# A four-stage transformer kernel: second attention in one product per head, additions moved between engines, a different preparation and heavier fillers

## The reference, cut to what matters

```python
x = x + tanh(g_xattn[0]) * attention_0(ctx, ctx, layernorm(x))   # 16 heads, softmax over the HEADS
x = x + tanh(g_ffn[0])   * ffn_0(layernorm(x))                   # silu(x Wg) * (x Wu), then Wd; hidden 768
x = x + tanh(g_xattn[1]) * attention_1(layernorm(x), ctx)        # 16 query heads, one k and v of width 16
x = x + tanh(g_ffn[1])   * ffn_1(layernorm(x))                   # x (W + low rank).T + b
# attention_1:
q = (x @ Wq) split into 16 heads of 16;  k, v = split(ctx @ Wkv, 2)
att = softmax(q k.T / 4, over the 120 context rows);  y = (att @ v) joined;  return y @ Wo
```

## Time and profile before

| | |
|---|---|
| median of three runs | 2813.01 us (2812.63 to 2813.55) |
| the profiled execution | 2812.17 us, of which its span is 2810.4 us |
| TensorE busy | 95% of the span |
| VectorE busy | 88% |
| ScalarE busy | 56% |
| GpSimd busy | 51% |
| granted TensorE clock over the span | 0.987 |

### The profile page before, as it was taken

How to read it: one execution, slowest core, us unless ns; L and a number is a source line. 1 busy time by engine, 2 the same in 40 slices (tenths; PEclk the granted TensorE clock), 3 DMA queues, 4 the chain that set the end, 5 groups by cost and what they waited for, 6 DMA issues and landing times.

```text
span 2810.4 us, 75822 instructions
## 1 busy us (share of the span) xinstructions
PE 2656.1 (95%) x30576; PEld 2278.9 (81%) x30576; DVE 2469.6 (88%) x4425; ACT 1563.9 (56%) x3125; POOL 1427.9 (51%) x1591
## 2 busy tenths in 40 slices
PE   3799999999999999999999999999999999999996
PEld 2688888888888888888888888888888888888884
DVE  4589999999999999999999999999999999999973
ACT  3355555555555555555555555555555555555553
POOL 1454465465455455456456446546545545545630
PEclk9799999999999999999999999999999999999997
DMA  2000000000000000000000000000000000000000
GB/s 76 24 22 25 26 25 29 23 27 28 21 28 27 21 30 25 21 30 25 25 27 25 25 26 27 28 21 27 28 21 30 25 21 30 25 21 30 25 16 9
DMA packets 74668, 73.15 MB, mean 26 GB/s; under 512 B 6907, under 2 KB 73745, under 8 KB 74642
## 3 DMA queue, kind: packets, MB, share of 16 engines
q1 hardware_dynamic: 74642, 72.80, 8.5%
HBM read 54.94 MB, written 16.78 MB: 26 GB/s over the span
## 4 chain that ended last, share of the span: by engine, by line
PE 36%; DVE 25%; POOL 24%; issue 6%; ACT 3%; DMA 2%; SPq 2%; POOLq 1%; DVEq 0%
POOL zt L345 8%; PE work L1081 8%; POOL h_lo L342 8%; PE work L1203 7%; PE work L1083 6%; PE work L1082 6%; DVE m L821 5%; POOL zt L349 4%; PE scores L1173 3%; DVE x L836 3%; POOL zt L352 2%; DVE y1f L833 2%; DVE e L830 2%; ACT e L509 2%; DMA x_ln<-xp 2%
## 5 line engine op out<-in xcount | busy, mean ns | idle before, releaser
L509 ACT ACTIVATE e<-scores 120x1024 f32<-120x1024 f32 x512 | 504.6, 1024 | 178.7 <-PE scores L1183 163.8
L342 POOL TENSOR_TENSOR h_lo<-h_f,h_hi 128x256 fp32r<-128x256 f32 x384 | 401.9, 1061 | 192.4 <-ACT h_hi L468 192.4
L1081 PE MATMUL work<-xt_hi_B,w_hi 128*128 128x256 f32 x1536 | 442.4, 288 | 0.9 <-DVE h_f L811 0.5
L1082 PE MATMUL work<-xt_lo_B,w_hi 128*128 128x256 f32 x1536 | 429.4, 280 | 0.0
L1083 PE MATMUL work<-xt_hi_B,w_lo 128*128 128x256 f32 x1536 | 428.5, 279 | 0.0
L830 DVE TENSOR_TENSOR e<-e,rz 120x2048 f32<-120x2048 f32 x128 | 383.8, 2998 | 2.2
L345 POOL TENSOR_TENSOR zt<-e 120x512 f32<-120x512 f32 x256 | 332.0, 1307 | 57.4 <-ACT e L509 57.4
L817 DVE TENSOR_REDUCE m<-scores 120x128 fp32r<-120x2048 f32 x128 | 293.3, 2291 | 27.6 <-PE scores L1173 24.3
L1081 PEld LDWEIGHTS work<-xt_hi_B,w_hi 128*128 128x128 f32 x1536 | 289.1, 188 | 11.8 <-DVE h_f L811 0.7
L1082 PEld LDWEIGHTS work<-xt_lo_B,w_hi 128*128 128x128 f32 x1536 | 289.5, 188 | 2.9
L1083 PEld LDWEIGHTS work<-xt_hi_B,w_lo 128*128 128x128 f32 x1536 | 289.1, 188 | 0.0
(11 more groups left out here) (192 smaller groups left out, 7323.1 us busy)
## 6 DMA issues: line engine op xcount, KB each, us to landing
x_ln<-xp SPq DMA_DIRECT2D x64, 256.0 KB, 2.7
x_res<-xp SPq DMA_DIRECT2D x64, 256.0 KB, 2.7
y<-y_out SPq DMA_DIRECT2D x64, 256.0 KB, 2.2
ctx_f_A<-cp SPq DMA_DIRECT2D x64, 128.0 KB, 2.5
ctx_f_C<-cp SPq DMA_DIRECT2D x64, 128.0 KB, 2.0
qm<-mT SPq DMA_DIRECT2D x256, 4.0 KB
e<-wi SPq DMA_DIRECT2D x3, 768.0 KB, 5.9
e<-wf SPq DMA_DIRECT2D x2, 512.0 KB, 3.6
```

Of the source, the lines that this page charges most:

```text
L342: return pool.tensor_tensor(h_lo[:, m, :], h_f[:, m % 2, :], h_hi[:, m, :].bitcast(F32), ALU.subtract)
L509: return act.activation(e[0:SC, c, 2 * h:2 * h + 2, :, :].rearrange("p a b n -> p (a b n)"), scores[0:SC, 2 * h:2 * h + 2, :].rearrange("p ...
L1081: pe.matmul(out, a_hi, b_hi_, start=first, stop=False, skip_group_check=parts)
L1082: pe.matmul(out, a_hi, b_lo_, start=False, stop=False, skip_group_check=parts)
```

## The change

- Second attention: the stationary operand is now `v1_one`, 16 columns of values and 16 of ones for 32 output partitions. One product per head gives values and sum together, so `attended1` has half of the products. The output has its queries along the free dimension, so VectorE turns each 128x512 bank by 32x32 blocks (`queries_to_rows`, two instructions), takes a reciprocal of 32 elements per partition, multiplies twice 256 elements (`weigh`), and turns the result back (`queries_to_columns`).
- Biases of two products (line 1086) are replaced by additions of a row by POOL (`add_row`, two per pass, 128x512). The last residual goes from VectorE to a copy by ScalarE (`f1_out`) and an addition by POOL (`last_residual`) one pass later. The low part `yC_lo` goes from VectorE to POOL. `keys0_odd` and `keys1_odd` go from VectorE to ScalarE. Keys and key scores run over 120 context rows, not 128.
- Order: `normalise(0)` stands at the end of VectorE's pass; `hidden(5)` stands between `reciprocal0(1)` and `normalise(1)`; on POOL `add_heads(1, 0)`, `add_heads(1, 1)` and `heads_total(1)` stand ahead of `hidden_lo(3)` to `hidden_lo(5)`; on TensorE `attended0(1)` stands behind `down(5)`, and `gate_up(5)` ends the pass. Banks are assigned anew.
- Preparation: four staging buffers, loads issued ahead, two of the low parts on POOL, the 128x4096 memsets gone, sixteen 128x128x512 products as a warm-up of TensorE.
- `DEPTH` = 4: 68 passes, of which 61 are full for TensorE. `skipped()` on TensorE is three products of 128x128x256.

The diff cut to its core:

```diff
-INIT_POOL = 8
+INIT_POOL = 9
 FIRST = 2
 STAGES_BEHIND = 0
-DEPTH = 3
+CONSTS = 7
+WARM = 16
+DEPTH = 4
...
-            def reciprocal1(cc):
-                return dve.reciprocal(y1f[:, cc * S:(cc + 1) * S], y1f[:, cc * S:(cc + 1) * S])
+            def queries_to_rows(cc, bank):
+                return dve.transpose(yz_q[:, cc, :, :, :].rearrange("p h q c -> p (h q c)"), bank[:, :])
+
+            def reciprocal1():
+                return dve.reciprocal(rz_q[:, :, :, :], yz_q[:, :, :, :, HD])
+
+            def weigh():
+                for cc in range(KC):
+                    last = dve.tensor_tensor(y_q[:, cc, :, :, :].rearrange("p q h d -> p h q d"), yz_q[:, cc, :, :, 0:HD],
+                                             rz_q[:, cc, :, :].unsqueeze(3).to_broadcast([P, 2, S // 32, HD]), ALU.mult)
+                return last
+
+            def queries_to_columns():
+                return dve.transpose(y1f[:, :, :].rearrange("p c q -> p (c q)"),
+                                     y_q[:, :, :, :, :].rearrange("p c q h d -> p (c q h d)"))
...
-            def attended1(bank, v, cc):
-                return per_head(bank, lambda g, par: v[0:SC, 32 * par:32 * par + 32], cc,
-                                lambda r, par: e1[0:SC, cc, r, par, :], 0, S)
+            def attended1(bank, cc):
+                for odd in range(2):
+                    for r in range(RG):
+                        last = pe.matmul(bank[32 * r:32 * r + 32, odd * S:(odd + 1) * S], v1_one[0:SC, :],
+                                         e1[0:SC, cc, r, odd, :], start=True, stop=True)
+                return last
 
             def skipped(bank):
-                return pe.matmul(bank[0:1, 0:1], ident[0:1, 0:1], ident[0:1, 0:1], start=True, stop=True, skip_group_check=True)
+                for n in range(3):
+                    last = pe.matmul(bank[:, 0:S], w_hi[:, 0:P], w_hi[:, 0:S], start=True, stop=True, skip_group_check=True)
+                return last
 
             def one_pass(t):
 
...
                 pe.wait_ge(s["A1_p"], t)
                 if live(t, 1):
-                    attended0(W[0], 1).then_inc(s["yA1_mm"], 1)
-                else:
-                    skipped(W[0]).then_inc(s["yA1_mm"], 1)
+                    attended0(W[2], 1).then_inc(s["yA1_mm"], 1)
+                else:
+                    skipped(W[2]).then_inc(s["yA1_mm"], 1)
+                if live(t, 3):
+                    attended1(W[3], 0).then_inc(s["yz0_mm"], 1)
+                else:
+                    skipped(W[3]).then_inc(s["yz0_mm"], 1)
                 pe.wait_ge(s["res_B"], t)
                 if live(t, 3):
-                    attended1(W[2], v1_pad, 0)
-                if live(t, 3):
-                    attended1(W[2], v1_pad, 1)
+                    attended1(W[1], 1).then_inc(s["yz1_mm"], 1)
...
+            def last_residual(x):
+                return pool.tensor_tensor(y_out[:, :, :], f1_out[:, :, :], x[:, :, :], ALU.add)
...
+                pool.wait_ge(s["ld_x_res"], 16 * (t - 1))
+                if live(t, 1):
+                    add_row(x_res, x_res, 0).then_inc(s["x_res_biased"], 1)
+                else:
+                    skipped().then_inc(s["x_res_biased"], 1)
+                pool.wait_ge(s["yC_hi"], t)
+                if live(t, 3):
+                    pool.tensor_tensor(y_lo["C"][:, :, :], y1f[:, :, :], y_hi["C"][:, :, :].bitcast(F32), ALU.subtract)\
+                        .then_inc(s["yC_lo"], 1)
...
+                dve.wait_ge(s["A1_z"], t)
+                if live(t, 1):
+                    reciprocal0(1).then_inc(s["A1_rz"], 1)
+                else:
+                    skipped().then_inc(s["A1_rz"], 1)
+                dve.wait_ge(s["G_a"], nth(1, 6, t))
                 dve.wait_ge(s["G_lo"], nth(0, 6, t))
                 if live(t, 2):
-                    hidden(4, W[1]).then_inc(s["G_h"], 1)
+                    hidden(5, W[3]).then_inc(s["G_h"], 1)
                 else:
                     skipped().then_inc(s["G_h"], 1)
-                dve.wait_ge(s["G_a"], nth(1, 6, t))
-                dve.wait_ge(s["G_lo"], nth(1, 6, t))
-                if live(t, 2):
-                    hidden(5, W[0]).then_inc(s["G_h"], 1)
-                else:
-                    skipped().then_inc(s["G_h"], 1)
-                dve.wait_ge(s["A1_z"], t)
-                if live(t, 1):
-                    reciprocal0(1).then_inc(s["A1_rz"], 1)
-                else:
-                    skipped().then_inc(s["A1_rz"], 1)
                 dve.wait_ge(s["A1_rz"], t)
                 if live(t, 1):
                     normalise(1).then_inc(s["A1_p"], 1)
...
+                dve.wait_ge(s["A0_z"], t)
+                if live(t, 0):
+                    reciprocal0(0).then_inc(s["A0_rz"], 1)
+                else:
+                    skipped().then_inc(s["A0_rz"], 1)
+                dve.wait_ge(s["A0_rz"], t)
+                if live(t, 0):
+                    normalise(0)
...
+            load_round(0)
+            sp.dma_start(graw[:, :], gates).then_inc(s["ld_gates"], 16)
+            load_round(1)
+            sp.dma_start(b_f[:, :], brow).then_inc(s["ld_cst"], 16)
             sp.dma_start(ident[:, :], cst[:, 0:P]).then_inc(s["ld_cst"], 16)
-            sp.dma_start(masks[:, :], cst[:, P:P + 2]).then_inc(s["ld_cst"], 16)
-            sp.dma_start(ones_pad[:, :], cst[:, P + 2:P + 66]).then_inc(s["ld_cst"], 16)
-            sp.dma_start(w_ctx[:, :], wc).then_inc(s["ld_cst"], 16)
-            sp.dma_start(graw[:, :], gates).then_inc(s["ld_cst"], 16)
-            sp.dma_start(b_f[:, :], brow).then_inc(s["ld_cst"], 16)
             sp.dma_start(ldT_s[:, :], ldT).then_inc(s["ld_cst"], 16)
             sp.dma_start(da_s[:, :], da).then_inc(s["ld_cst"], 16)
             sp.dma_start(luT_s[:, :], luT).then_inc(s["ld_cst"], 16)
             sp.dma_start(uaT_s[:, :], uaT).then_inc(s["ld_cst"], 16)
-            for r, (name, n) in enumerate(ROUNDS):
-                if r >= 2:
-                    sp.wait_ge(s["w_lo"], r - 1)
-                src = wi[:, SEG[name]:SEG[name] + n] if r < 3 else wf[:, SEG[name] - SEG["q0"]:SEG[name] - SEG["q0"] + n]
-                dst = stage[r % 2][:, 0:n]
-                sp.dma_start(dst.bitcast(I32) if r < 3 else dst, src).then_inc(s[f"ld_w{r % 2}"], 16)
-            sp.wait_ge(s["b_split"], 2)
-            sp.wait_ge(s["bias_zero"], 1)
-            sp.dma_start(bias_k[0:1, :].bitcast(F32), b_hi.bitcast(F32)).then_inc(s["ld_bias"], 16)
-            sp.dma_start(bias_k[1:2, :].bitcast(F32), b_lo.bitcast(F32)).then_inc(s["ld_bias"], 16)
+            load_round(2)
+            sp.dma_start(w_ctx[:, :], wc).then_inc(s["ld_cst"], 16)
+            load_round(3)
+            sp.wait_ge(s["w_lo"], 1)
+            load_round(4)
+            sp.wait_ge(s["w_lo_pool"], 1)
+            load_round(5)
```

More of the change, by code:

```diff
@@ L386, in one_pass @@
                     skipped().then_inc(s["A1_z"], 1)
+                pool.wait_ge(s["G_hi"], nth(0, 6, t))
+                if live(t, 2):
+                    hidden_lo(3).then_inc(s["G_lo"], 1)
+                else:
+                    skipped().then_inc(s["G_lo"], 1)
                 pool.wait_ge(s["G_hi"], nth(1, 6, t))
@@ L438, in one_pass @@
                     skipped().then_inc(s["G_lo"], 1)
+                pool.wait_ge(s["G_hi"], nth(5, 6, t))
+                if live(t, 1):
+                    hidden_lo(2).then_inc(s["G_lo"], 1)
+                else:
+                    skipped().then_inc(s["G_lo"], 1)
             for t in range(FIRST, FIRST + DEPTH):
@@ L694, in one_pass @@
                     exponential(e0, 1, 0).then_inc(s["A1_exp"], 1)
+                else:
+                    skipped().then_inc(s["A1_exp"], 1)
+                act.wait_ge(s["A1_sub"], nth(1, 2, t))
+                if live(t, 0):
+                    exponential(e0, 1, 1).then_inc(s["A1_exp"], 1)
                 else:
@@ new lines, in _ @@
+            low_part("down", HC * D, 2).then_inc(s["w_lo"], 1)
+            st = stage[1][:, 0:KC * D]
+            dve.wait_ge(s["ld_w5"], 16)
+            dve.wait_ge(s["li"], 1)
+            dve.tensor_tensor(st, W[2][:, :], st, ALU.add).then_inc(s["li_sum"], 1)
+            dve.wait_ge(s["li_sum"], 1)
+            dve.tensor_scalar(st, st, tg[:, 3:4], None, ALU.mult).then_inc(s["w_scaled"], 1)
+            low_part("wo0", 2 * KC * D, 4).then_inc(s["w_lo"], 1)
+            low_part("f1", KC * D, 5).then_inc(s["w_lo"], 1)
@@ L913, in one_pass @@
+                dve.wait_ge(s["yz0_mm"], t)
+                if live(t, 3):
+                    queries_to_rows(0, W[3]).then_inc(s["yz0"], 1)
+                else:
+                    skipped().then_inc(s["yz0"], 1)
+                dve.wait_ge(s["yz1_mm"], t)
                 if live(t, 3):
-                    reciprocal1(1).then_inc(s["rzC1"], 1)
+                    queries_to_rows(1, W[1]).then_inc(s["yz1"], 1)
                 else:
-                    skipped().then_inc(s["rzC1"], 1)
```

(32 more changed lines are left out.)

655 lines of the change are left out of this document (315 added, 340 removed), and 8 rows, old and new, of the table per_pass.

## The result

The changed kernel takes 2828.8 us (median of 4 runs, 2827.6 to 2831.7) where the kernel before takes 2812.8 (2811.4 to 2813.6): ratio 1.0061, 95% interval 1.0048 to 1.0075. It is slower by about 16 us. The profiled execution has a span of 2825.8 us, 15.4 us more than before.

A forecast was written before the change was run, and what follows sets the result against it. A pass was taken to be one trip round a loop of engines: 41.67 - 0.6 + 1.6 - 0.2 - 0.4 = 42.1 us, +25 us in 61 passes. With ends of -12: 2826 us, range 2808 to 2846.

The forecast's parts named there:

- the ends: Preparation and partial passes at front and end: -18 - 7 + 13 = -12 us together, between 0 and -20.
- Steps 1 and 2: From the start of scores0(0), S, to z of half 1: first stretch unchanged, then z at +20.0, gain 0.6 us.
- Step 3: From z of half 1 to the residual of B: hidden_lo(5) waits for normalise(1), residual at S+25.4, +1.6 us.
- Step 4: Residual of B to the queries of C: 6.3 us where before 6.5, transposes at 0.65 each.
- rival C: Block transposes on VectorE take 1.2 us, not 0.65: +1.65 us a pass, +100 us, 2926 us; chance 0.13.
- Step 5: Queries of C to the next S: 2.9, 3.35, 1.05 instead of 1.3, then 3.0 us; gain 0.4.
- TensorE's "36": TensorE's work in one changed pass, put at 36 us, with room in the 42.1 us.
- VectorE's 35: VectorE's work in one changed pass, put at 35 us, with room in the 42.1 us.
- Rival D: Fillers in partial passes fail: clock stays low and they cost twice 0.36, another +15 us, 2841 us; chance 0.07.
- the 6 and 1 us: Partial passes with fillers at full clock: perhaps 6 us lost by three at the end, 1 at the front.
- the price of those products: End of the stream: 38 skipped steps of three products, 38 x 0.36 = 13.7 us, with hops some 15.
- Rival A: Exclusion not as suggested, or hidden_lo(5) ahead of normalise(1): residual at +23.75, 40.4 us a pass, 2723 us; chance 0.15.

The follow-up runs named there:

- e2: Changed kernel with the order of the kernel before for the steps of chunks 3 to 5, rest of the change kept: 2745.2 us, ratio 0.9764.
- e6: Changed kernel with normalise(1) done for half of the heads only, the other half left unnormalised: 2733.1 us, ratio 0.972.
- e10: e7 with one more VectorE transpose of 128x512 from PSUM, into memory that nothing reads then: 2732.9 us, ratio 0.9714.
- e4: Changed kernel with TensorE's skipped() back to one 1x1 product in place of three of 128x128 by 128x256: 2829.2 us, ratio 1.0059.
- e7: e2 with hidden_lo(3) done by VectorE ahead of hidden(5), in place of POOL: 2698.4 us, ratio 0.9597.

## Why the prediction came out as it did

The time (2826 against 2828.8) and the sign were right, and the mechanism that I named for the loss, `hidden_lo(5)` shut out by `normalise(1)` and TensorE waiting for it, is shown by e2 and e6. But the loop's number was close by two errors that partly cancelled, a walk that was too long and a clock that I left out; and the total was closer still because the loop cost 8 us more than I had put and the ends gained 5 more. That 2826 came out within 3 us was luck.

- Steps 1 and 2: right. z of half 0 at S+11.1 (I said 11.0), both `hidden_lo` done at 12.5 (12.4), `normalise(0)` from 12.1 to 14.6 (12.4 to 14.7), the first additions of half 1 stretched from 2.5 to 3.85 us, z of half 1 at 19.7 (20.0).
- Step 3: right in kind, 0.5 us too long. `hidden(5)` took its 0.36 in front of `normalise(1)`, which ran from 20.9 to 23.25; `hidden_lo(5)` ended at 23.8 (24.4), the residual started at 24.9 (25.4). Of the 0.5, 0.3 came from z, and most of the rest from the last part of `hidden_lo(5)` behind the normalise, 0.57 us where I had put 0.75. TensorE's idle time there was 1.74 us, I had said 2.2.
- What the step left out is what that idle time does. I counted it as free: "attended0(1) and attended1(0) are behind it", and no more. In 22 of 61 passes it brought half of the clock for 3.4 us and 1.27 us of time, 28 us in all. The earlier trace rows had shown clocks of 0.75 where TensorE is less busy, but I had looked at them only for the ends.
- Step 4: the transposes at 0.65 each, right: 0.65 us from one to the next here, 0.59 in e10, on the path. By the Trainium skill (Vector Engine (DVE) Microarchitecture Reference, 3.8), which has the transpose sustain one element per cycle and lane, my estimate was 0.53; the measurement decides, some 0.1 more, and rival C's 1.2 is out. The way from the residual to the queries of C took 6.5 us, not 6.3, as before the change: VectorE's cheaper reciprocal was spent on the transposes.
- Step 5: right. 2.93 and 3.38 us to the key scores, 1.02 to the queries of A, 3.05 to the next S.
- So the short pass is 41.75, where I had 42.1: 0.35 too much, 21 us in 61 passes; the clock makes it 42.21 on average. The work of the engines I had less well, without harm to the walk: TensorE's "36" should have been 40.7 less 2.4, 38.3, and is 38.7; VectorE's 35 is 33.5.
- The ends: -17 us, I had -12, inside my range of 0 to -20. VectorE's first step of pass 0 stands at 31.1 us (I said 28; before 46.4), 15 us earlier, and the exponential of pass 1 comes 17.6 earlier. From pass 1 to pass 3 took 3.1 us less than before. The end took 3.6 more, where I had +13 less 6. Rival D's 15 us are out. Of my own terms, the 6 and 1 us gained by a better clock are borne out by e4 (6.0 at the end and 2.4 at the front, with the products there); too large was the price of those products, 13.7, since e4 without them takes as long.
- Rival A, had `hidden_lo(5)` gone ahead, was 40.4 us and 2723. e2 makes it so and gives 40.87 and 2745, since its order also puts `hidden_lo(3)` ahead of z; e7, without that, gives 40.09 and 2698. The exclusion stands (e6), as the 2.77 us of the earlier trace rows had suggested.

One table sums up the loop. The distance from the start of the residual of B to the next S is the same in four kernels, and what differs is when the residual can start:

| kernel | residual starts | a pass (short) | from the residual on |
|---|---|---|---|
| before | S+24.4 | 41.67 | 17.3 |
| after | S+24.9 | 41.75 | 16.9 |
| e6, half of normalise(1) | S+23.8 | 40.69 | 16.9 |
| e2, old order | S+24.0 | 40.87 | 16.9 |
| e7, hidden_lo(3) on VectorE too | S+23.2 | 40.09 | 16.9 |

The second part became shorter by 0.4 us a pass, all of it behind the queries of C (step 5); up to there the new attention with its transposes takes as long as the old one. The new order around `normalise(1)` took 0.5 in the first part, and the idle time that it left on TensorE brought the lower clock. With e2's order the whole change is worth 2812 - 2745 = 67 us.

## What to carry to other kernels

An operation that runs elsewhere is not free if both engines want the same ports: put GpSimd's short steps that somebody waits for ahead of VectorE's long operation with two inputs in SBUF, and look at which of the two comes first, since in these traces the other waited for all of it. Where the chain goes round several engines, a few steps of 0.4 to 0.7 us in the wrong order cost more (82 us with the clock) than the whole change brings with the right one (67 us), although VectorE has 282 us less to do. And idle time of TensorE is to be read together with the granted clock behind it, and not as slack only: four throw-away products of 0.1 us each brought back 26 us.

## What the runs showed of the hardware that I had not expected

- The granted clock fell to half for 3.4 us behind an idle time of TensorE of 1.62 to 2.38 us, in 21 to 43 of 61 passes, inside loops in which it is busy for over 90% of the time. With 0.45 us of that idle time filled (1.27 left) it never fell.
- The exclusion of VectorE and GpSimd holds in both directions: GpSimd's 0.7 us became 2.3 beside a normalise, and two VectorE products of 0.76 us became 1.89 beside a GpSimd addition of 1.28 that had started 0.01 us before them.
- TensorE at a lower clock at the end of the stream (0.83 for 45 us, then 0.50 for 43 us in e4) came with two partial passes that are 6.0 us longer, and the throw-away products that kept the clock up made the way from there to the end 5.1 us longer.
